# Layer turn of a graph network: old rows and biases of four tiles added by one wide product each

## The chip, the cores and the metric

The kernel runs on 1 core of one Trainium2 chip. The metric is the device time of one launch in microseconds (us), the median of the runs shown: before the change 7408.9 us (3 runs, 7406.33 to 7413.53).

## The reference, cut to what matters

The kernel computes four stacked graph layers on 6250 nodes with 128 channels and 100000 edges. The change touches the first of them, L0, a graph transformer of four rounds (`N_LAYERS = 4`):

```python
h = x @ Wn + bn
for l in range(N_LAYERS):
    Q = h @ WQ[l] + bQ[l]; K = h @ WK[l] + bK[l]; V = h @ WV[l] + bV[l]
    scores = jnp.sum(Q[dst] * K[src], axis=-1) * scale
    e = jnp.exp(scores - seg_max[dst])
    messages = jax.ops.segment_sum((e / seg_sum[dst])[:, None] * V[src], dst, num_segments=n)
    out = messages @ WO[l] + bO[l]
    h = _layernorm(h + out, ln_g[l], ln_b[l])
return h @ Wout + bout
```

All arithmetic here is float32. A node with no incoming edge gets no share of bV, so the bias that is added to h is bO for all nodes and bV @ WO for nodes with edges only.

## The kernel before, in words

**Tiles.** The 6250 rows are 49 tiles of 128 nodes (`T`), in an order that the kernel made itself (`k.perm`, `L.perm`). `k.h` holds the rows of the layer, `k.acc` the sums that the edge pass made (columns 0 to 127) and their denominators (column 128). Columns 129 to 256 of `k.acc` are free in this mode and are named `k.marks` (L3571); a row pair of them is used here.

**Order of the whole.** L3581: a loop of three rounds over `edge_pass` and `layer_turn` (so turns 1 to 3 are the same code), then one more `edge_pass` and one `layer_turn` with `last=True` (turn 4). Everything behind it (`place_rest`, `near_edges`, the later layers) follows in order. Each function is a stage: it ends in `close_stage` (L101), a reset of the DMA semaphores on POOL and a barrier of all engines. So whatever a turn takes longer or shorter moves the end of the kernel.

**A turn.** `layer_turn` (L2720) goes through the 49 tiles in 13 groups of `GB = 4` (L2686; the last group has one tile). For group g:

1. ACT `weigh` (L2832) multiplies the sums by the reciprocal denominators into `a`.
2. PE transposes the four tiles of `a` into `turned_ps` (L2787), ACT copies them to `at` (L2849).
3. PE adds up `sum_ps[g % 2]` (L2799 to L2801), per tile three products of 128 columns: the identity times the old rows, the marks (two rows: "has an edge" and "one") times `k.add2` (two rows: bV @ WO and bO), and `at` times `wvo`, the product of WV and WO.
4. DVE takes mean and variance (L2914, L2917), ACT the root (L2842), DVE the scale (L2905, L2907), ACT the normalised rows (L2858), DVE applies gain and offset (L2930, L2932) and stores them to `k.h` (`stored`).
5. In turns 1 to 3 POOL scatters each stored tile to the table in HBM with one indirect DMA (L2963). In turn 4 POOL has no such work; it gathers the 49 tiles of x with indirect DMAs from the start of the turn (L2954).
6. PE transposes the new rows (L2815), ACT copies them (L2867), PE multiplies them by `w2` (L2823), DVE adds the bias (L2947, in turn 4 L2943 and L2945).

The engines run these steps in queues written out by hand: in step i of the loop PE does the transposes of group i, the sums of i-1, the transposes of new rows of i-3 and the products of i-4. The order on PE is fixed, so a wait in the sums holds all that is behind it.

**The start of a turn.** SP loads the marks of all tiles with one DMA into two partitions of `k.acc` (L2756; `marked`). PE transposes the weights and makes bV @ WO as one row (L2762), DVE copies it into row 0 of `k.add2` (L2881; `raw`), and row 1, bO, was fetched during the edge pass by `fetch_layer` on ACT's queue (L2707). PE's first sum waits for `marked` and `made` (L2793, L2794).

**Names.** `own` is a helper that counts DVE's own instructions, so that DVE can wait for its own writes. `FETCHED` (L2687) is the number of DMAs that SP waits for at L2447, at the end of the edge pass.

Of the kernel before, what the change touches and what calls it, by code (L numbers as in the profile page):

```python
# [23 lines left out]
P = 128  # L24
# [3 lines left out]
NPAD = T * P  # L28
# [2655 lines left out]


GB = 4  # L2686
FETCHED = {False: 10, True: 8}  # L2687
NGB = -(-T // GB)


def group_tiles(g):
# [4 lines left out]
def fetch_layer(act, m, k, I, l, last):  # L2696

    def matrix(n, j):
        return I[f"L0_gnn_{n}"][ds(j, 1)].rearrange("a i j -> (a i) j")

    def column(n, j):
        return I[f"L0_gnn_{n}"][ds(j, 1)].rearrange("a (p n) -> (a p) n", n=1)

    act.dma_start(k.raw["WV"][:], matrix("WV", l)).then_inc(m["fetched"], 16)
    act.dma_start(k.raw["WO"][:], matrix("WO", l)).then_inc(m["fetched"], 16)
    act.dma_start(k.bv[:], column("bV", l), allow_slow_non_contiguous=True).then_inc(m["fetched"], 16)
    act.dma_start(k.add2[1:2], I["L0_gnn_bO"][ds(l, 1)]).then_inc(m["fetched"], 16)  # L2707
    for n, o in (("ln_g", k.gb), ("ln_b", k.bb)):
        act.dma_start(o[:], I[f"L0_gnn_{n}"][ds(l, 1)].rearrange("a n -> (a n)").partition_broadcast(P)).then_inc(m["fetched"], 16)
    if last:  # L2710
        act.dma_start(k.w1[:], I["L0_gnn_Wout"]).then_inc(m["fetched"], 16)
        act.dma_start(k.b1[:], row(I["L0_gnn_bout"])).then_inc(m["fetched"], 16)
        return
    act.dma_start(k.raw["WQ"][:], matrix("WQ", l + 1)).then_inc(m["fetched"], 16)
    act.dma_start(k.raw["WK"][:], matrix("WK", l + 1)).then_inc(m["fetched"], 16)
    act.dma_start(k.bq[:], column("bQ", l + 1), allow_slow_non_contiguous=True).then_inc(m["fetched"], 16)
    act.dma_start(k.bk[:], column("bK", l + 1), allow_slow_non_contiguous=True).then_inc(m["fetched"], 16)


def layer_turn(nc, k, last, x_d):  # L2720

    made = ["WV"] if last else ["WV", "WQ", "WK"]
    W2 = P if last else P + 1
    with ExitStack() as s:
        m = open_stage(nc, s, ["own", "shares", "raw_ps", "raw", "made_ps", "made", "spread_ps", "weighed", "turned_ps", "turned",
                               "summed_ps", "stat", "rooted", "scale", "normed", "stored", "rows_ps", "rows", "out_ps", "out_taken",
                               "scattered", "marked"] + [f"kept{g}" for g in range(NGB if last else 0)])
        wt = {n: buf(nc, s, f"wt_{n}", [P, P + 1]) for n in made}
        wvo = buf(nc, s, "wvo", [P, P])
        wz = buf(nc, s, "wz", [P, P + 1])  # L2730
        bz = buf(nc, s, "bz", [1, P + 1])
        bias = buf(nc, s, "lt_bias", [P, W2])
# [20 lines left out]
        with nc.Block() as block:  # L2753
            @block.sync
            def _(sp):
                sp.dma_start(k.marks[0:2], k.marks_d.rearrange("r (t p) -> r t p", p=P)).then_inc(m["marked"], 16)  # L2756

            @block.tensor
            def _(pe):
                for r, n in enumerate(made):  # L2760
                    pe.transpose(w_ps[:, r, :], k.raw[n][:], k.ident[:])
                pe.matmul(w_ps[0:1, 3, :], k.bv[:], k.raw["WO"][:], start=True, stop=True).then_inc(m["raw_ps"], 1)  # L2762
                pe.wait_ge(m["raw"], 2)
                pe.matmul(made_ps[:, 0, :], wt["WV"][:, 0:P], k.raw["WO"][:], start=True, stop=True).then_inc(m["made_ps"], 1)

                def next_weights():
# [13 lines left out]
                for i in range(NGB + 4):  # L2780
# [8 lines left out]
                    if 0 <= i - 1 < NGB:  # L2789
                        g = i - 1  # L2790
                        pe.wait_ge(m["turned"], g + 1)
                        if g == 0:
                            pe.wait_ge(m["made"], 1)  # L2793
                            pe.wait_ge(m["marked"], 16)  # L2794
                        if g >= 2:
                            pe.wait_ge(m["normed"], g - 1)
                        for j, t in enumerate(group_tiles(g)):
                            o = sum_ps[g % 2][:, j, :]
                            pe.matmul(o, k.ident[:], k.h[:, t, :], start=True, stop=False)  # L2799
                            pe.matmul(o, k.marks[0:2, t, :], k.add2[0:2], start=False, stop=False)  # L2800
                            mm = pe.matmul(o, at[g % 2][:, j, :], wvo[:], start=False, stop=True)  # L2801
                        mm.then_inc(m["summed_ps"], 1)
                        if g == 0:
                            next_weights()
                        if g == 1:
                            spread_bias()
# [63 lines left out]
            def _(dve):  # L2870
# [7 lines left out]
                dve.reciprocal(share[:], den[:]).then_inc(m["shares"], 1)  # L2878
                dve.wait_ge(m["raw_ps"], 1)
                dve.tensor_copy(wt["WV"][:, 0:P], w_ps[:, 0, :]).then_inc(m["raw"], 1)  # L2880
                dve.tensor_copy(k.add2[0:1], w_ps[0:1, 3, :]).then_inc(m["raw"], 1)  # L2881
                dve.wait_ge(m["made_ps"], 1)
                dve.tensor_copy(wvo[:], made_ps[:, 0, :]).then_inc(m["made"], 1)
                for r, n in enumerate(made[1:]):
# [65 lines left out]
            if last:  # L2950
                @block.gpsimd
                def _(pool):
                    for t in range(T):
                        pool.indirect_dma_start(k.x[:, t, :], None, x_d, bass.IndirectOffsetOnAxis(k.perm[:, t:t + 1], 0),  # L2954
                                                bounds_check=N - 1, oob_is_err=False).then_inc(m[f"kept{t // GB}"], 16)

            if not last:
                @block.gpsimd
                def _(pool):
                    for t in range(T):  # L2960
                        if t % GB == 0:
                            pool.wait_ge(m["stored"], t // GB + 1)
                        pool.indirect_dma_start(k.table_d, bass.IndirectOffsetOnAxis(k.perm[:, t:t + 1], 0), k.h[:, t, :], None  # L2963
                                                ).then_inc(m["scattered"], 16)
                    pool.wait_ge(m["scattered"], 16 * T)
# [291 lines left out]
def take_nodes(nc, k, I, deg, dn, list_d):  # L3257

    with ExitStack() as s:
# [39 lines left out]
        with nc.Block() as block:  # L3299
# [60 lines left out]
            def _(dve):  # L3360
# [13 lines left out]
                dve.wait_ge(m["marks_ps"], 1)  # L3374
                dve.tensor_copy(rows[:], small[0:T, 2, :]).then_inc(m["marks"], 1)
                dve.memset(k.acc[:, :, 0:P + 1], 0.0)
                dve.memset(k.add2[:], 0.0)
                dve.memset(k.x[:], 0.0)
                dve.wait_ge(m["loaded"], 16 * 7)
                for i, parts in enumerate((k.parts2, k.parts3)):  # L3380
# [105 lines left out]
def gnn_kernel(nc, I, out_d):  # L3486
    with ExitStack() as c:
# [84 lines left out]
        with ExitStack() as s:  # L3572
            k.raw = {n: buf(nc, s, f"raw_{n}", [P, P]) for n in ("WQ", "WK", "WV", "WO")}
            k.bq = buf(nc, s, "bq", [P, 1])
            k.bk = buf(nc, s, "bk", [P, 1])
            k.bv = buf(nc, s, "bv", [P, 1])
            k.add2 = buf(nc, s, "add2", [P, P])
            k.gb = buf(nc, s, "ln_g", [P, P])
            k.bb = buf(nc, s, "ln_b", [P, P])
            take_nodes(nc, k, I, L.deg, dn, listed[0])  # L3580
            with nc.Fori(0, k.layers - 1) as l:  # L3581
                edge_pass(nc, k, "attend", k.table_d, NPAD, P, *listed[0:3], dn.sched, fetch=(I, l, False), sort=(so, l), dn=dn)
                layer_turn(nc, k, False, I["x"])
            edge_pass(nc, k, "attend", k.table_d, NPAD, P, *listed[0:3], dn.sched, fetch=(I, k.layers - 1, True), sort=(so, k.layers - 1), dn=dn)
            layer_turn(nc, k, True, I["x"])
        place_rest(nc, k, so, L.sched, chunks)
        near_edges(nc, k, so, chunks, sweeps)
        with ExitStack() as s:
# [61 lines left out]
```

## Time and profile before

| | before |
|---|---|
| median of 3 runs | 7408.9 us |
| lowest, highest | 7406.33, 7413.53 us |
| span of the profiled execution | 10258.0 us |
| its mean granted TensorE clock | 0.709 of full speed |
| PE busy | 5437.6 us, 53% of the span |
| weight loads (PEld) busy | 4358.8 us, 42% |
| DVE busy | 4372.6 us, 43% |
| ACT busy | 2633.3 us, 26% |
| POOL busy | 4650.8 us, 45% |
| instructions | 129339 |

The profiled execution has no time of its own beside its span; the span is that of 129339 recorded instructions and is 38% above the median of the runs. No engine is busy for much more than half of it: the kernel is a chain of stages with different limits. A float32 product shows as two matmul records and two weight loads on PE (a transpose as one), so "x8" in a timeline row of L2823 is four products. The granted clock is given as a share of full speed: 1.00 is 2.4 GHz, 0.50 is 1.2 GHz.

### The profile page before, as it was taken

The numbers are of one execution on the slowest core, as the hardware profiler recorded it, in microseconds if no ns is written. First come the engines' busy times: TensorE is split into PE (matmuls) and PEld (weight loads), VectorE is DVE, ScalarE is ACT, GpSimd is POOL, SyncE is SP. The second block draws the span as 40 slices with busy tenths as digits, with TensorE's granted clock in tenths as the row PEclk, the third lists the DMA queues.
The fourth block names the chain that finished last, engine by engine and source line by source line (L and its number), as shares of the span: only waits on it lengthen the run. The fifth ranks groups of instructions, "written<-read, shape, count | busy, mean of one in ns | idle before, by whom it ended". The sixth has DMA issues, their size and how long they took to land. (4 is left out here: it accounts for less than half of the span.)

```text
span 10258.0 us, 129339 instructions
## 1 busy us (share of the span) xinstructions
PE 5437.6 (53%) x28962; PEld 4358.8 (42%) x28963; DVE 4372.6 (43%) x13513; ACT 2633.3 (26%) x7476; POOL 4650.8 (45%) x4878
## 2 busy tenths in 40 slices
PE   4404555554555555455645454444444455886888
PEld 3203444443444444444534343322222234776777
DVE  7503444424444334444334443344444454444444
ACT  0102222232222222222322222213333333333111
POOL 1473444434444444444444445244445444444554
PEclk8556777767777667777667777666666666887888
DMA  4202222112222122222122222122222213222222
GB/s 155 69 0 60 57 56 59 54 47 56 57 55 56 42 61 55 57 58 56 33 68 57 55 57 54 32 85 67 68 68 70 69 49 91 61 62 56 65 66 58
DMA packets 404676, 615.62 MB, mean 60 GB/s; under 512 B 213466, under 2 KB 255993, under 8 KB 403884
## 3 DMA queue, kind: packets, MB, share of 16 engines
q0 software_dynamic: 169952, 363.29, 13.1%
q1 hardware_dynamic: 211126, 200.20, 7.0%
q10 hardware_dynamic: 23130, 47.29, 1.4%
q14 instruction: 345, 2.83, 0.1%
q8 instruction: 123, 2.02, 0.1%
HBM read 528.32 MB, written 82.09 MB: 60 GB/s over the span
## 5 line engine op out<-in xcount | busy, mean ns | idle before, releaser
L1973 POOL DMA_INDIRECT rows<-table_d,meta x2432 | 2308.2, 949 | 1648.2 <-ACT weighted_rows L2140 835.2
L2037 PE MATMUL ps_total<-weighted_rows,ident 128*128 128x129 f32 (+1 forms) x6464 | 1700.6, 417 | 2122.2 <-issue 1604.1
L2037 PEld LDWEIGHTS ps_total<-weighted_rows,ident 128*128 128x128 f32 x6464 | 1329.3, 270 | 2529.7 <-issue 2423.2
L2369 DVE SCALAR_TENSOR_TENSOR prod<-rows,q_rows 128x129 f32<-128x129 f32 x2432 | 695.4, 294 | 1510.9 <-issue 1346.1
L1973 POOL DMA_INDIRECT rows<-pairs_d,meta x800 | 769.9, 962 | 781.3 <-DVE once_weighted L2429 526.6
L2073 PE MATMUL dense_sums<-x_rows,dense_power_t 128*128 128x129 f32 x3528 | 593.5, 317 | 662.8 <-issue 293.2
L2158 ACT COPY dense_power_t<-dense_turned 128x512 f32<-128x512 f32 x504 | 264.8, 525 | 2371.5 <-PE dense_turned L2064 1658.7
L2073 PEld LDWEIGHTS dense_sums<-x_rows,dense_power_t 128*128 128x128 f32 x3528 | 528.6, 227 | 703.6 <-issue 580.6
L2140 ACT ACTIVATE weighted_rows<-rows,power 128x129 f32<-128x129 f32 x2432 | 733.3, 389 | 18.4 <-PE ps_total L2037 14.6
L1532 POOL DMA_INDIRECT tile_rows<-table_d,tile_halves x441 | 416.2, 944 | 427.3 <-PE tile_sums L1783 294.2
L2193 ACT ACTIVATE weighted_rows<-once_weighted,of_relation 128x136 f32<-128x136 f32 x1600 | 488.0, 393 | 454.6 <-DVE once_weighted L2429 422.7
L1532 POOL DMA_INDIRECT tile_rows<-made_d,tile_halves x441 | 416.7, 945 | 378.0 <-PE tile_sums L1783 245.6
L1979 POOL DMA_INDIRECT list_out_d<-sort_stretch,sort_idx x72 | 74.8, 1039 | 1111.7 <-DVEq L2321 1111.7
L2250 DVE CUSTOM_DVE_ANT_0 dense_masked<-dense_scores,dense_masked,dense_least 128x896 f32<-128x896 f32 x252 | 289.7, 1150 | 499.6 <-issue 229.0
L1773 PE MATMUL tile_sums<-near_rows,sums 128*128 128x129 f32 x2352 | 366.3, 293 | 170.1 <-issue 166.7
L2064 PE MATMUL dense_turned<-ident,dense_masked 128*128 128x128 f32 x1764 | 318.3, 301 | 217.4 <-issue 138.2
L2372 DVE TENSOR_TENSOR src_store<-rows,q_rows 128x128 f32<-128x128 f32 x800 | 209.9, 291 | 516.3 <-issue 499.3
L2053 PE MATMUL dense_scores<-sums,dense_asked_t 128*128 128x512 f32 x512 | 317.2, 704 | 161.0 <-DVE dense_least L2250 61.7
L1773 PEld LDWEIGHTS tile_sums<-near_rows,sums 128*128 128x128 f32 x2352 | 314.1, 202 | 202.7 <-issue 201.4
L1783 PE MATMUL tile_sums<-tile_rows,sums 128*128 128x129 f32 x1764 | 339.2, 357 | 103.9 <-issue 103.1
L2064 PEld LDWEIGHTS dense_turned<-ident,dense_masked 128*128 128x128 f32 x1764 | 225.3, 153 | 340.4 <-issue 199.2
L1783 PEld LDWEIGHTS tile_sums<-tile_rows,sums 128*128 128x128 f32 x1764 | 314.6, 267 | 128.5 <-issue 128.4
(700 smaller groups left out, 9515.6 us busy)
## 6 DMA issues: line engine op xcount, KB each, us to landing
dense_masked<-dense_masks_d SPq DMA_DIRECT2D x252, 448.0 KB
rows<-table_d,meta POOLq DMA_INDIRECT x2432
dense_masks_d<-unmasked ACTq DMA_DIRECT2D x9, 3136.0 KB
src_store<-near_window_d SPq DMA_DIRECT2D x50, 384.0 KB
near_window<-near_window_d SPq DMA_DIRECT2D x48, 384.0 KB
rows<-pairs_d,meta POOLq DMA_INDIRECT x800
tile_rows<-table_d,tile_halves POOLq DMA_INDIRECT x441
tile_rows<-made_d,tile_halves POOLq DMA_INDIRECT x441
```

The costliest lines, as they stand in the source:

```text
L1532: pool.indirect_dma_start(rows[b][:, c, 0:P], None, table_d, bass.IndirectOffsetOnAxis(meta[:, t, c:c + 1], 0)).then_inc(got[b] if t < T - ...
L1773: pe.matmul(total[:, q, 0:P + 1], spare[:, q, c, :], near_rows[q][:, c, :], start=(c == 0), stop=False)
L1783: mm = pe.matmul(total[:, q, 0:P + 1], spare[:, q, NEAR + c, :], rows[t % RB][:, c, :], start=False, stop=(c == FARC - 1))
L1973: pool.indirect_dma_start(rows[q][:, j, 0:width], None, table_d, bass.IndirectOffsetOnAxis(meta[q][:, j, number:number + 1], 0)).then_inc( ...
L2037: mm = pe.matmul(total[:, q, ds(part, 1), 0:W].rearrange("p a w -> p (a w)"), k.ident[:], wide[:, j % WS, :], start=False, stop=True, skip ...
L2053: pe.matmul(dense_ps[:, 0, :].rearrange("p (t c) -> p t c", c=P), asked_t[:], xt[:, t0:t0 + 4, :], start=True, stop=True)
L2064: mm = pe.transpose(power_ps[:, j * P:(j + 1) * P], masked[u % 2][:, c * P:(c + 1) * P], k.ident[:])
L2073: mm = pe.matmul(sum_ps[:, 0:P + 1], power_t[h][:, j, :], k.x1[:, u * UNIT + 4 * h + j, :], start=(h == 0 and j == 0), stop=(h == 1 and j ...
L2140: ins = act.activation(wide[:, j, :], rows[q][:, j, :], ACT.Copy, scale=power[q][:, 0, j + 1:j + 2])
L2193: ins = act.activation(wide[:, j % WS, r * HW:(r + 1) * HW], once[:, j].rearrange("p h d -> p (h d)"), ACT.Copy, scale=of_relation[q][:, j ...
L2250: dve.tensor_tensor_reduce(masked[u % 2][:], dense_ps[:].rearrange("p b c -> p (b c)")[:, 0:UW], masked[u % 2][:], 1.0, least[:, u:u + 1], ...
L2369: own(dve.scalar_tensor_tensor(prod[:, j % 2, :], rows[q][:, j, :], -1.0, query, ALU.mult, ALU.mult, accum_out=score[:, j, :]))
```

## The change

Old rows and biases of the four tiles of a group are added by one product of 512 columns each, into the four quarters of one PSUM bank. For the biases this takes a block matrix: tile j of the group has its two marks in partitions 32j and 32j+1, and `add4` holds the two bias rows of tile j in the same partitions, in columns of tile j alone; all else in it is zero. The contraction runs over `BROWS` = 98 partitions. `add4` and the marks are therefore set to zero by POOL at the start of each turn, then SP loads marks and bO with nine DMAs in place of one (and of the one on ACT's queue in the edge pass), and DVE copies the bV @ WO row four times. The product with `wvo` stays one per tile.

```diff
-FETCHED = {False: 10, True: 8}
+FETCHED = {False: 9, True: 7}
+BROWS = 32 * (GB - 1) + 2
...
-    act.dma_start(k.add2[1:2], I["L0_gnn_bO"][ds(l, 1)]).then_inc(m["fetched"], 16)
...
+        add4 = buf(nc, s, "lt_add", [P, GB, P])
...
             @block.sync
             def _(sp):
-                sp.dma_start(k.marks[0:2], k.marks_d.rearrange("r (t p) -> r t p", p=P)).then_inc(m["marked"], 16)
+                sp.wait_ge(m["unmarked"], 2)
+                of_group = k.marks_d[:, 0:(NGB - 1) * GB * P].rearrange("r (g j p) -> r j g p", j=GB, p=P)
+                for j in range(GB):
+                    sp.dma_start(k.marks[32 * j:32 * j + 2, 0:NGB - 1, :], of_group[:, j]).then_inc(m["marked"], 16)
+                    sp.dma_start(add4[32 * j + 1:32 * j + 2, j, :], I["L0_gnn_bO"][ds(l, 1)]).then_inc(m["marked"], 16)
+                sp.dma_start(k.marks[0:2, NGB - 1, :], k.marks_d[:, (NGB - 1) * GB * P:NPAD]).then_inc(m["marked"], 16)
...
-                pe.matmul(w_ps[0:1, 3, :], k.bv[:], k.raw["WO"][:], start=True, stop=True).then_inc(m["raw_ps"], 1)
-                pe.wait_ge(m["raw"], 2)
+                pe.matmul(w_ps[0:BROWS, 3, :], k.bv[:].to_broadcast([P, BROWS]), k.raw["WO"][:], start=True, stop=True).then_inc(m["raw_ps"], 1)
+                pe.wait_ge(m["raw"], 1)
...
-                            pe.wait_ge(m["marked"], 16)
+                            pe.wait_ge(m["marked"], 16 * (2 * GB + 1))
+                            pe.wait_ge(m["raw"], 2)
                         if g >= 2:
                             pe.wait_ge(m["normed"], g - 1)
-                        for j, t in enumerate(group_tiles(g)):
-                            o = sum_ps[g % 2][:, j, :]
-                            pe.matmul(o, k.ident[:], k.h[:, t, :], start=True, stop=False)
-                            pe.matmul(o, k.marks[0:2, t, :], k.add2[0:2], start=False, stop=False)
-                            mm = pe.matmul(o, at[g % 2][:, j, :], wvo[:], start=False, stop=True)
+                        n = len(group_tiles(g))
+                        pe.matmul(sum_ps[g % 2][:, 0:n, :], k.ident[:], k.h[:, g * GB:g * GB + n, :], start=True, stop=False,
+                                  skip_group_check=True)
+                        pe.matmul(sum_ps[g % 2][:, 0:n, :], k.marks[0:BROWS, g, :], add4[0:BROWS, 0:n, :], start=False, stop=False,
+                                  skip_group_check=True)
+                        for j in range(n):
+                            mm = pe.matmul(sum_ps[g % 2][:, j, :], at[g % 2][:, j, :], wvo[:], start=False, stop=True, skip_group_check=True)
...
-                dve.tensor_copy(k.add2[0:1], w_ps[0:1, 3, :]).then_inc(m["raw"], 1)
+                for j in range(GB - 1):
+                    if j == 0:
+                        dve.wait_ge(m["unmarked"], 2)
+                    own(dve.tensor_copy(add4[32 * j:32 * j + 1, j, :], w_ps[32 * j:32 * j + 1, 3, :]))
+                own.wait()
+                dve.tensor_copy(add4[BROWS - 2:BROWS - 1, GB - 1, :], w_ps[BROWS - 2:BROWS - 1, 3, :]).then_inc(m["raw"], 1)
...
              @block.gpsimd
             def _(pool):
+                    pool.memset(add4[:], 0.0).then_inc(m["unmarked"], 1)
+                    pool.memset(k.marks[:, 0:NGB, :], 0.0).then_inc(m["unmarked"], 1)
```

Beside this `k.add2` and its clearing before the first layer are dropped, and `layer_turn` is given the inputs and the layer's number.

## Rows read from the trace of the kernel before

**Rows 1.** Windows: the four turns, each up to the next stage (busy us, clock, DMA).

```profile
2117.90:2235.80 117.90, 96.11 (x503) 76.45 (x503) 45.24 (x176) 50.62 (x139) 48.16 (x49) 0.77 0.09 29
3561.00:3682.70 121.70, 102.48 (x503) 82.27 (x503) 45.55 (x177) 50.60 (x139) 47.94 (x49) 0.71 0.08 28
5012.00:5130.00 118.00, 102.94 (x503) 82.83 (x503) 45.55 (x177) 51.26 (x139) 47.88 (x49) 0.71 0.08 28
6449.90:6600.40 150.50, 98.79 (x497) 79.54 (x497) 52.84 (x184) 51.37 (x139) 48.84 (x49) 0.68 0.08 22
```

**Rows 2.** Windows inside turns 1 and 3: PE, PEld, DVE, ACT, POOL busy; clock.

```profile
2134.00:2143.00 9.00, 9.00 (x30) 6.76 (x30) 1.49 (x11) 3.15 (x9) 0.00 (x0) 0.50 0.00 1
2158.00:2164.00 6.00, 6.00 (x43) 5.03 (x42) 3.40 (x14) 4.04 (x12) 3.67 (x5) 1.00 0.12 39
...
5079.00:5089.00 10.00, 10.00 (x37) 8.21 (x36) 2.56 (x13) 3.73 (x11) 4.96 (x5) 0.50 0.12 39
```

**Rows 3.** Timeline, PE in turn 1 at clock 1.00: one group (start us, us).

```profile
2158.76 0.39 PE L2799 MATMUL lt_sum<-h_rows,ident 128*128 128x128 f32 x2
2159.08 0.48 PE L2800 MATMUL lt_sum<-add,sums 2*128 2x128 f32 x2
2159.82 0.39 PE L2799 MATMUL lt_sum<-h_rows,ident 128*128 128x128 f32 x2
2163.42 1.06 PE L2823 MATMUL lt_out<-wz,lt_ht 128*128 128x129 f32 x8
2164.75 0.39 PE L2799 MATMUL lt_sum<-h_rows,ident 128*128 128x128 f32 x2
```

**Rows 4.** Timeline, PE in turn 1 at clock 0.50: two tiles of group 0.

```profile
2124.49 0.64 PE L2799 MATMUL lt_sum<-h_rows,ident 128*128 128x128 f32 x2
2126.36 0.63 PE L2799 MATMUL lt_sum<-h_rows,ident 128*128 128x128 f32 x2
```

**Rows 5.** Timeline, PE: products of 512 columns in edge passes, fast and slow.

```profile
5331.49 1.13 PE L2053 MATMUL dense_scores<-sums,dense_asked_t 128*128 128x512 f32 x2 [1.31 <-DVE dense_least L2250]
5332.46 0.81 PE L2055 MATMUL dense_scores<-sums,dense_asked_t 128*128 128x384 f32 x2
...
2289.70 2.08 PE L2053 MATMUL dense_scores<-sums,dense_asked_t 128*128 128x512 f32 x2 [1.53 <-DVE dense_least L2250]
2291.57 1.49 PE L2055 MATMUL dense_scores<-sums,dense_asked_t 128*128 128x384 f32 x2
```

**Rows 6.** POOL's scatters of turns 1 to 3 (line L2963: duration; idle time before).

```profile
L2963 POOL DMA_INDIRECT table_d<-h_rows,perm_in x147: 963/969/1187, 2144.8 to 5120.8; - x147
  issue: 38.6, 120
```

**Rows 7.** Start of a turn: DMA issues, a POOL memset, a DMA's landing (last number, us).

```profile
2117.92 0.78 SPq L2756 DMA_DIRECT2D sums<-marks_d  x1
L2707 ACTq DMA_DIRECT2D add<-in_L_gnn_bO x4: 486/488/536, 816.5 to 5149.9; - x4
L3302 POOL MEMSET dense_same<- 128x1600 f32 x1 | 1.4, 1431 | 7.8 <-POOLq L3564 7.8
tile_packed<-list_out_d SPq DMA_DIRECT2D x28, 31.5 KB, 2.2
```

**Rows 8.** Timeline, turn 4: a PE record, POOL's last gather, DVE's return.

```profile
6495.94 0.37 PE L2801 MATMUL lt_sum<-wvo,lt_at 128*128 128x128 f32 x1 [2.43 <-issue]
...
6513.21 0.99 POOL L2954 DMA_INDIRECT x_rows<-in_x,perm_in  x1 [0.30 <-issue]
...
6519.77 0.89 DVE L2914 BATCH_NORM_STATS2 lt_stats<-lt_sum 128x6 f32<-128x128 f32 x4 [52.01 <-remote]
```

**Rows 9.** Timeline, DVE: a late resumption in turn 1; the stage after turn 3.

```profile
2206.02 0.89 DVE L2914 BATCH_NORM_STATS2 lt_stats<-lt_sum 128x6 f32<-128x128 f32 x4 [7.04 <-DMA em_x<-in_x]
...
5129.98 0.10 DVE L1905 MEMSET rows<- 128x16 f32 x2 [1.63 <-PEq L104]
```

More of the change, by code:

```diff
@@ L2717, in fetch_layer, with layer_turn @@
     act.dma_start(k.bk[:], column("bK", l + 1), allow_slow_non_contiguous=True).then_inc(m["fetched"], 16)
-def layer_turn(nc, k, last, x_d):
+def layer_turn(nc, k, I, l, last):
+    x_d = I["x"]
     made = ["WV"] if last else ["WV", "WQ", "WK"]
@@ L2726, in layer_turn @@
                                "summed_ps", "stat", "rooted", "scale", "normed", "stored", "rows_ps", "rows", "out_ps", "out_taken",
-                               "scattered", "marked"] + [f"kept{g}" for g in range(NGB if last else 0)])
+                               "scattered", "marked", "unmarked"] + [f"kept{g}" for g in range(NGB if last else 0)])
         wt = {n: buf(nc, s, f"wt_{n}", [P, P + 1]) for n in made}
         wvo = buf(nc, s, "wvo", [P, P])
+        add4 = buf(nc, s, "lt_add", [P, GB, P])
         wz = buf(nc, s, "wz", [P, P + 1])
@@ L2959, in _ @@
                 def _(pool):
+                    pool.memset(add4[:], 0.0).then_inc(m["unmarked"], 1)
+                    pool.memset(k.marks[:, 0:NGB, :], 0.0).then_inc(m["unmarked"], 1)
                     for t in range(T):
@@ L3376, in _ @@
                 dve.memset(k.acc[:, :, 0:P + 1], 0.0)
-                dve.memset(k.add2[:], 0.0)
                 dve.memset(k.x[:], 0.0)
@@ L3576, in gnn_kernel @@
             k.bv = buf(nc, s, "bv", [P, 1])
-            k.add2 = buf(nc, s, "add2", [P, P])
             k.gb = buf(nc, s, "ln_g", [P, P])
@@ L3582, in gnn_kernel @@
                 edge_pass(nc, k, "attend", k.table_d, NPAD, P, *listed[0:3], dn.sched, fetch=(I, l, False), sort=(so, l), dn=dn)
-                layer_turn(nc, k, False, I["x"])
+                layer_turn(nc, k, I, l, False)
             edge_pass(nc, k, "attend", k.table_d, NPAD, P, *listed[0:3], dn.sched, fetch=(I, k.layers - 1, True), sort=(so, k.layers - 1), dn=dn)
-            layer_turn(nc, k, True, I["x"])
+            layer_turn(nc, k, I, k.layers - 1, True)
         place_rest(nc, k, so, L.sched, chunks)
```

## The prediction, made before the changed kernel was run

> **What bounds the kernel now.** I read the page first: no engine is busy for much over half of the span, so the question is which one sets the pace inside the four turns. The windows over each turn [rows 1] give 117.9, 121.7, 118.0 and 150.5 us, 508 us of the profiled span of 10258.0. PE is busy for 96 to 103 us of each, no other engine for more than 53. The windows inside a turn [rows 2] show PE busy in every microsecond, at clock 0.50 (1.2 GHz) 16 to 25 us into turn 1 and at 1.00 (2.4 GHz) 40 us into it; in turn 3 it stood at 0.50 once more, 67 us in. So in most of a turn PE's own work sets the pace.
>
> What that work is, the timeline shows. At clock 1.00 the first product of group 4 starts at 2158.76 and that of group 5 at 2164.75 [rows 3]: a period of 5.99 us. One tile of sums takes 2159.82 - 2158.76 = 1.06 us, four take 4.24, and the other 1.75 us are the two sets of transposes and the four products of L2823. At clock 0.50 a tile takes 1.87 us [rows 4], a group of sums 7.48.
>
> Two other things bound it. POOL's scatters in turns 1 to 3 take 0.969 us and 38.6 / 120 = 0.32 us of issue before each [rows 6], so 4 x 1.29 = 5.16 us a group: PE can't get faster than that for long, since the turn ends only when all 49 are out. And DVE comes back late now and then: at 2206.02 it had been idle for 7.04 us and the row names a DMA, not PE, whose sums it takes up [rows 9]. In turn 4 it is far stronger: while POOL gathers without a pause (to 6514.2), PE issues one record at a time, 2.43 us of idle before one of 0.37, and DVE comes back at 6519.77 after 52.01 us [rows 8]. I take both for late instructions; the rows show the lateness, not the cause.
>
> **The change part by part, for one full group.** It removes six of twelve products. The identity product becomes one of 512 columns. Edge passes have such products: 5332.46 - 5331.49 = 0.97 us fast, 2291.57 - 2289.70 = 1.87 us slow [rows 5]. The marks' product has 98 rows in place of 2; there is no such row. Its ends are 0.97 (its columns, rows being free) and 1.64 us (four narrow ones at 2159.82 - 2159.08 = 0.74 less one identity product's 0.32, so about 0.41 each, as now); I take 0.97, since the wide row has 128 partitions. The four products with wvo then stand one behind another as those of L2823 do, 1.06 us for four [rows 3], slow twice that, 2.12. Sum of a group, fast: 0.97 + 0.97 + 1.06 = 3.00 us for 4.24, so 1.24 less; slow: 1.87 + 1.87 + 2.12 = 5.86 for 7.48, 1.62 less. A whole fast group becomes 4.75 us on PE, and in turns 1 to 3 POOL's 5.16 is longer: there the gain is 5.99 - 5.16 = 0.83.
>
> **The start of a turn.** Added on the path to `marked`: POOL clears 512 + 13 x 128 = 2176 elements a partition, at 1431 / 1600 ns each [rows 7] 1.95 us. SP waits for it, with nothing else queued behind. Then nine issues: before, one of 98 row pieces took 0.78 us, one of a single row 0.49 [rows 7]. Four with 24 pieces I put at 0.6, four of bO at 0.49, the last at 0.5: 4.9 us (ends 4.4 and 7.0, nine times either row). Landing 2.2 us, from a load of 31.5 KB [rows 7] (ends 1.5, were it a third less, and 4.4, were it double under POOL's gathers). From 2117.92 that gives 2127.0, where the first sum started at 2124.49 [rows 4]: 2.5 us late (ends 1.3 and 6.8). Behind this wait PE holds the transposes of group 2, then ACT and DVE; all shift by it.
>
> Costed at nothing: DVE's four row copies and their wait for the memsets (till about 2119.9; they end some 1.2 us later, 3 us ahead of PE's first sum even as it was; uncovered they would cost that 1.2), the 98-column weight load for bV @ WO, and the DMA that leaves ACT's queue (0.49 us, in the edge pass, off its path). The clearing in turn 4 stands in front of POOL's gathers and moves the starved stretch by its 1.95 us; the marks' wait is hidden behind that stretch.
>
> **Sum.** Turns 1 to 3, each: +2.5 at the start; three slow groups -4.9 (from 2124.49 on, at 7.48 and some 1.6 for the rest, they reach to about 2152); nine fast full groups, of which the first five gain 0.83, -4.2, and four in the second half gain nothing, since there DVE's returns set the pace (if they don't, 3.3 more). Together -6.6, three times -19.8. Turn 4: +1.95, one slow group -1.6, eight fast ones at 1.24, -9.9 (POOL is done by then): -9.6. In all -29.4 us, against the profiled span 10258.0 a fall to 10228.6. That span is 38% above the median of the runs; the durations inside a turn are those of engines, so I carry the difference over one to one: 7408.9 - 29.4 = 7379.5, rounded to 7380. A measurement can tell about 0.2%, 15 us, from no change.
>
> **Rivals.** *(a) The wide product is used in full*: fewer instructions on PE end the late returns, all nine fast groups gain, the delay is 2.0. Turns 1 to 3: -4.9 - 7.5 + 2.0 = -10.4 each; in all -41, 7368. For it: PE issues 72 products fewer per turn. Against: the late engine in rows 9 is DVE, whose instructions don't get fewer. Chance 0.16.
>
> *(b) A new bound takes it*: POOL's scatters, now back to back, hold the engines' instructions as the gathers do in turn 4 [rows 8]. PE's gain at full clock is lost in turns 1 to 3, and the start costs 4.5: -0.4 each; only turn 4's -9.6 is left, -11, 7398. For it: the 52.01 us of rows 8. Against: in turn 1 POOL was 61% busy in the window of 6 us in which nothing was late [rows 2]. The Trainium skill, page "Runtime: NRT & Kernel Launch", section "Instruction fetch mechanics", says that each sequencer fetches its next block of instructions through a DMA queue of its own and that this is mostly hidden. By the rule alone this case should cost next to nothing and (a) be right; rows 8 and 9 speak against its "hidden". Chance 0.26.
>
> *(c) Slower: PE's clock.* It was 0.50 until some 25 us into turn 1 and again late in turn 3 [rows 2]. PE now gets pauses that it had not: the wait for `marked`, and 5.16 - 4.75 = 0.4 us in each group behind POOL. If it then stays low, a group takes 5.86 + 2 x 1.75 = 9.4 us where I count 5.16, 4.2 more. The forecast's 29.4 are gone after 7 such groups over all turns, and 15 us on the far side after 10.5. With four a turn: 16 x 4.2 = 67, so +38, 7447. For it: turn 3 did so by itself. Against: 0.4 in 5.16 leaves PE 92% busy. The Trainium skill, "TensorE: Matmul & The Clock Gate", section "HAM oscillation — how this bites in real kernels", says that pauses between bursts of products send the clock back to half. The trace has one such fall in turn 3, and none in the rows of full work. Chance 0.10.
>
> *(d) The change doesn't do what it says*: what a product costs lies in its columns, which stay the same, and the wide ones take as long as four narrow ones, 4.24 in all. Then only the starts count: 3 x 2.5 + 1.95 = +9.5, 7418. Against: rows 5, 0.97 for 512 columns beside 4 x 0.32 for the identity's four. Chance 0.06.
>
> **How the numbers follow.** The forecast has 0.42, with a range of its own of 7370 to 7391 (start and second half at either end). Faster by over 15 us (below 7394): the forecast, (a) and a fifth of (b), 0.63. Within 0.2%: the rest of (b), (d), 0.27. Slower: (c), 0.10. The range 7361 to 7406 takes in (a) and (b) with the bounds of the start and leaves out (c), (d) and the outermost part of (a).
>
> **What the changed profile would show.** The lines of L2799 and L2800 have 104 records each for the 52 groups (392 now), with 512 columns. The period of the first products at clock 1.00 is 5.1 to 5.2 us in turns 1 to 3, and 4.75 in turn 4. POOL's waits for h_rows get short, its waits for issue stay at 0.32. The first sum of a turn starts 9 us after the turn and not 6.6. The windows of rows 1 become some 111, 115, 111 and 141 us. I am wrong if the periods stay near 6 (then (b) or (d), told apart by the duration of the wide record), if the first sum is later than 11 us, or if clock 0.50 stands in more than the first four groups (then (c)).

## The result, and the profile after

The changed kernel took 7312.5 us, the median of 4 runs (7307.9 to 7316.4), beside 7411.2 us (7406.3 to 7417.9, 4 runs) for the kernel before: a ratio of 0.986 with an interval of 0.9848 to 0.9872, 98.7 us less. The forecast was 29.4 less, so the sign was right and the gain over three times as large. A single launch is now and then drawn out by hundreds of us or more (8272.1 us among the four of start_alone, whose median without it is 7311.3, and 9887.5 among the ten of rows_64), and the ratios leave such launches out.

The profiled execution of before that stands ahead of the prediction (span 10258.0 us) was a drawn-out one. A second one of the same kernel, below named *before again*, has a span of 7381.4 us. What follows compares with that one. First the top of the page of the changed kernel.

```profile
span 7314.8 us, 128253 instructions
PE 4737.9 (65%) x28386; PEld 3901.0 (53%) x28387; DVE 4310.6 (59%) x13524; ACT 2620.7 (36%) x7476; POOL 4676.6 (64%) x4886
```

Windows of the changed kernel, the four turns and the first 10 us of sums in turn 1, which answer to [rows 1, 2] (stretch; its length; busy us and instructions of PE, PEld, DVE, ACT, POOL; granted clock; DMA share; GB/s):

```profile
1691.80:1785.20 93.40, 64.00 (x359) 47.25 (x359) 46.16 (x180) 50.47 (x139) 51.85 (x51) 0.80 0.11 36
2689.20:2781.80 92.60, 63.83 (x359) 47.35 (x359) 46.42 (x181) 50.46 (x139) 51.15 (x51) 0.80 0.11 36
3687.70:3776.80 89.10, 63.92 (x359) 47.72 (x359) 46.45 (x179) 50.42 (x139) 51.89 (x51) 0.81 0.11 37
4681.90:4760.60 78.70, 65.25 (x354) 48.04 (x355) 54.79 (x188) 48.97 (x139) 51.81 (x51) 0.86 0.15 42
...
1698.00:1703.00 5.00, 5.00 (x12) 2.67 (x11) 0.00 (x0) 1.76 (x5) 0.00 (x0) 0.50 0.01 3
1703.00:1708.00 5.00, 5.00 (x28) 3.45 (x28) 2.37 (x14) 2.80 (x9) 0.00 (x0) 0.95 0.01 2
```

The same of before again, the four turns, then the stretch of turn 1 in which the clock rose, one of turn 2 25 to 34 us into it, and the one behind that, in which the clock rose:

```profile
1687.00:1790.10 103.10, 84.96 (x503) 68.69 (x503) 45.12 (x177) 51.82 (x139) 47.71 (x49) 0.85 0.10 33
2696.00:2807.40 111.40, 92.75 (x503) 74.76 (x503) 45.11 (x177) 51.92 (x139) 47.68 (x49) 0.78 0.09 30
3713.20:3821.40 108.20, 92.72 (x503) 74.72 (x503) 45.07 (x176) 51.93 (x139) 47.67 (x49) 0.79 0.09 31
4722.20:4830.90 108.70, 97.73 (x498) 78.77 (x499) 52.82 (x185) 51.59 (x139) 49.69 (x49) 0.74 0.12 31
...
1703.00:1707.00 4.00, 4.00 (x23) 3.05 (x21) 0.34 (x2) 3.15 (x9) 0.00 (x0) 0.88 0.00 0
2721.00:2730.00 9.00, 9.00 (x33) 7.21 (x32) 2.73 (x12) 3.52 (x11) 3.93 (x4) 0.50 0.08 29
2730.00:2734.00 4.00, 4.00 (x22) 3.17 (x21) 1.89 (x8) 3.85 (x11) 1.74 (x2) 0.83 0.05 16
```

The turns add up to 431.4 us before and 353.8 after: 77.6 less. All else together is 11.0 us longer after (6961.0 for 6950.0), so the spans differ by 66.6. In these two profiles and those of the eight other kernels below, this rest lies between 6950 and 6967 us and the turns add up to between 351 and 459, so nearly all that tells one kernel from another lies in the turns. PE's busy time in a turn fell by 21 to 33 us, POOL's rose by some 4 at most: the gain is PE's. It comes in two ways. The clock rose 5 us after the first sum (the window from 1703.00 to 1708.00 has 0.95 in the mean), where in turn 2 of before again it was still 0.50 in the window that ends 34 us into the turn, with PE busy in all of it. And a group at full clock is shorter, as PE's timeline in turn 1 after the change shows, group 0 at clock 0.50 and a later one at 1.00, answering to [rows 3, 4] (start, us, operation):

```profile
1698.52 2.05 PE L2807 MATMUL lt_sum<-h_rows,ident 128*128 128x512 f32 x2
1700.35 1.91 PE L2809 MATMUL lt_sum<-lt_add,sums 98*128 98x512 f32 x2
1702.06 1.76 PE L2812 MATMUL lt_sum<-wvo,lt_at 128*128 128x128 f32 x8
...
1730.01 1.02 PE L2807 MATMUL lt_sum<-h_rows,ident 128*128 128x512 f32 x2
1730.87 1.02 PE L2809 MATMUL lt_sum<-lt_add,sums 98*128 98x512 f32 x2
1731.73 1.05 PE L2812 MATMUL lt_sum<-wvo,lt_at 128*128 128x128 f32 x8
1732.63 0.60 PE L2826 MATMUL lt_rows<-ident,h_rows 128*128 128x128 f32 x4
```

From start to start: 0.86 + 0.86 + 0.90 = 2.62 us for a group's sums, where [rows 3] gave 4.24. The period of a group is 4.38 us (DVE takes up the sums of two groups in turn 1 at 1724.07 and 1728.45, with 0.89 us of waiting for PE before each).

The start of turn 1 in the timeline (POOL's clearing, the first and last of SP's nine issues, PE's second set of transposes), answering to [rows 7]:

```profile
1692.17 0.53 POOL L2978 MEMSET lt_add<- 128x512 f32 x1 [16.44 <-issue]
1692.63 1.50 POOL L2979 MEMSET sums<- 128x1664 f32 x1
1694.16 0.27 SPq L2762 DMA_DIRECT2D sums<-marks_d  x1
...
1696.80 0.25 SPq L2764 DMA_DIRECT2D sums<-marks_d  x1
...
1697.50 1.11 PE L2795 MATMUL lt_turned<-ident,lt_a 128*128 128x128 f32 x4 [1.85 <-ACT lt_a L2843]
```

The first sum starts 6.7 us into the turn (1698.52 - 1691.8), and 6.6 in before again (1693.59 - 1687.0): the marks' longer way cost next to nothing. POOL's scatters of turn 1, answering to [rows 6]:

```profile
L2983 POOL DMA_INDIRECT table_d<-h_rows,perm_in x49: 965/972/1519, 1710.7 to 1774.2; - x49
  issue: 14.6, 48
```

From the start of the first scatter (1710.7) to that of the last (1774.2) are 63.5 us and 48 steps. A step of 0.972 + 14.6 / 48 = 1.276 gives 61.2, and five scatters that took longer (up to 1.519 for 0.972) give the rest. The only idle time before a scatter is that of its issue, so POOL has no gap left. Turn 1 is 18.9 us to the first scatter, 63.5 to the start of the last and 11.0 from there to the end, 93.4 in all. PE's groups come every 4.38 us, faster than POOL's 4 x 1.276 = 5.10, so in turns 1 to 3 the bound is now POOL's, as forecast.

### The profile page after: what moved, and what is told of

Read it like the earlier page. It is cut to its first block and busy times, and to the rows that moved or that the text cites. A ratio compares the mean times of both kernels' runs of the same rounds, so it can differ in the third digit from the quotient of the medians.

```text
span 7314.8 us, 128253 instructions
## 1 busy us (share of the span) xinstructions
PE 4737.9 (65%) x28386; PEld 3901.0 (53%) x28387; DVE 4310.6 (59%) x13524; ACT 2620.7 (36%) x7476; POOL 4676.6 (64%) x4886
## 3 DMA queue, kind: packets, MB, share of 16 engines
q8 instruction: 119, 1.95, 0.1%
## 5 line engine op out<-in xcount | busy, mean ns | idle before, releaser
L2037 PE MATMUL ps_total<-weighted_rows,ident 128*128 128x129 f32 (+1 forms) x6464 | 1425.4, 380 | 652.7 <-ACT weighted_rows L2193 484.8
L2037 PEld LDWEIGHTS ps_total<-weighted_rows,ident 128*128 128x128 f32 x6464 | 1179.9, 235 | 897.7 <-issue 725.3
L2073 PE MATMUL dense_sums<-x_rows,dense_power_t 128*128 128x129 f32 x3528 | 622.0, 328 | 557.1 <-DVE dense_rows L2260 521.6
L2073 PEld LDWEIGHTS dense_sums<-x_rows,dense_power_t 128*128 128x128 f32 x3528 | 558.9, 238 | 598.2 <-issue 590.9
L2146 ACT ACTIVATE dense_shrink<-dense_least 128x1 f32<-128x1 f32 x252 | 74.0, 294 | 749.8 <-DVE dense_least L2250 749.8
L2064 PEld LDWEIGHTS dense_turned<-ident,dense_masked 128*128 128x128 f32 x1764 | 241.0, 159 | 163.7 <-ACT dense_power_t L2158 91.4
L1758 PE MATMUL near_gathered<-q_rows,near_hot 128*128 128x128 f32 x2352 | 275.7, 278 | 73.7 <-DVE near_hot L1622 73.7
L1758 PEld LDWEIGHTS near_gathered<-q_rows,near_hot 128*128 128x128 f32 x2352 | 271.4, 195 | 74.2 <-DVE near_hot L1622 67.9
L1991 PE MATMUL ps_total<-nothing,ident_bf 128*128 128x387 bf16 x160 | 67.6, 427 | 359.9 <-DVE nothing L2231 345.4
L1758 PE MATMUL near_gathered<-x_rows,near_hot 128*128 128x128 f32 x2352 | 275.5, 278 | 31.9 <-DVE near_hot L1622 31.9
```

Source lines behind the costliest of these rows:

```text
L1758: mm = pe.matmul(gathered[:, h, at:at + P], near_hot[i][:, c % 2, j, :], table[:, WIDE * c + j, 0:P], start=(j == 0), stop=(j == WIDE - 1) ...
L2037: mm = pe.matmul(total[:, q, ds(part, 1), 0:W].rearrange("p a w -> p (a w)"), k.ident[:], wide[:, j % WS, :], start=False, stop=True, skip ...
L2064: mm = pe.transpose(power_ps[:, j * P:(j + 1) * P], masked[u % 2][:, c * P:(c + 1) * P], k.ident[:])
L2073: mm = pe.matmul(sum_ps[:, 0:P + 1], power_t[h][:, j, :], k.x1[:, u * UNIT + 4 * h + j, :], start=(h == 0 and j == 0), stop=(h == 1 and j ...
```

## The experiments

Each is an edit of the kernel before unless said otherwise. "Turns" are the four turns of its profiled execution. In the rows `sums` is the buffer of the marks and `add` is `k.add2`.

**before_again.** The kernel before, unchanged.

> The kernel before, unchanged, profiled once more, since its first profile had a span of 10258 us where the changed kernel's is 7314.8. Clock theory (the wide products let TensorE's clock rise earlier, and that is the larger part of the 98.7 us): a span near 7410, turns 1 to 3 of 110 to 118 us each, and clock 0.50 for at least the first 25 us of PE's sums in every turn, although PE has no pause. Work theory (the gain is the products' own time, and the profile of before was drawn out elsewhere): the clock is at 1.00 within 10 us of the first sum, and a group takes 6.0 us from then on.

Its run was 7382.9 us, its turns 103.1, 111.4, 108.2, 108.7. In turn 4 nothing is starved: DVE's waits are PE's sums, as this row of its timeline shows, where [rows 8] had 52.01 us.

```profile
4788.51 0.89 DVE L2914 BATCH_NORM_STATS2 lt_stats<-lt_sum 128x6 f32<-128x128 f32 x4 [1.77 <-PE lt_sum L2801]
```

So [rows 8, 9] belong to that one drawn-out execution and not to the kernel. The group's period at full clock is 5.99 us here too, so [rows 3] do belong to it.

**start_alone.** The changed kernel with its marks, block matrix and start, but twelve products of 128 columns per group, in the old order.

```diff
-                        pe.matmul(sum_ps[g % 2][:, 0:n, :], k.ident[:], k.h[:, g * GB:g * GB + n, :], ...)
-                        pe.matmul(sum_ps[g % 2][:, 0:n, :], k.marks[0:BROWS, g, :], add4[0:BROWS, 0:n, :], ...)
+                        for j, t in enumerate(group_tiles(g)):
+                            o = sum_ps[g % 2][:, j, :]
+                            pe.matmul(o, k.ident[:], k.h[:, t, :], start=True, stop=False)
+                            pe.matmul(o, k.marks[0:BROWS, g, :], add4[0:BROWS, j, :], start=False, stop=False)
+                            mm = pe.matmul(o, at[g % 2][:, j, :], wvo[:], start=False, stop=True)
```

> The new start (clearing, nine DMAs, block matrix, marks' product over 98 rows) with products of 128 columns only, twelve a group as before. Clock theory: nothing raises the clock, so the start's cost alone shows: 2 to 10 us slower than before, turns at 0.50 as long as in before. If the 98 rows in place of 2 were what raises the clock: 30 us or more faster. Work theory: 2 to 10 us slower.

Measured: 7314.2 us, ratio 0.9874 (0.9847 to 0.9901); turns 91.6, 92.6, 88.7, 77.7, period 4.45. That is the full change's time with none of its wide products for the old rows and biases. PE's timeline at clock 1.00:

```profile
1715.53 0.39 PE L2809 MATMUL lt_sum<-h_rows,ident 128*128 128x128 f32 x2
1715.75 0.39 PE L2810 MATMUL lt_sum<-lt_add,sums 98*128 98x128 f32 x2
1715.98 0.39 PE L2811 MATMUL lt_sum<-wvo,lt_at 128*128 128x128 f32 x2
1716.20 0.39 PE L2809 MATMUL lt_sum<-h_rows,ident 128*128 128x128 f32 x2
```

Every narrow product takes 0.22 to 0.23 us, a tile 0.67, where it was 1.06 in [rows 3]. Not only the bias product got cheaper, which now has 98 rows, but also the two of 128 rows on either side of it, which did not change. So what was paid for before stands between products, not in them.

**rows_wide.** Only the old rows by one wide product; the biases stay two rows.

```diff
+                        pe.matmul(sum_ps[g % 2][:, 0:n, :], k.ident[:], k.h[:, g * GB:g * GB + n, :], start=True, stop=False, ...)
                         for j, t in enumerate(group_tiles(g)):
-                            pe.matmul(o, k.ident[:], k.h[:, t, :], start=True, stop=False)
```

> Only the old rows as one product of 512 columns per group; start and marks' products as before (nine products a group). Clock theory: the clock rises nearly as early as in the changed kernel; 50 to 90 us faster than before. Work theory: PE's own saving alone, (4 x 0.32 - 0.97) to 0.5 us a group, 52 groups: 15 to 30 us faster.

Measured: 7404.6 us, ratio 0.9996 (0.9984 to 1.0008): nothing. Its timeline at clock 1.00:

```profile
1742.37 1.02 PE L2798 MATMUL lt_sum<-h_rows,ident 128*128 128x512 f32 x2
1743.32 0.48 PE L2802 MATMUL lt_sum<-add,sums 2*128 2x128 f32 x2
1743.73 0.49 PE L2803 MATMUL lt_sum<-wvo,lt_at 128*128 128x128 f32 x2
1746.56 0.60 PE L2817 MATMUL lt_rows<-ident,h_rows 128*128 128x128 f32 x4
```

The last row is the first transpose behind the group. From start to start a group's sums take 1746.56 - 1742.37 = 4.19 us, where twelve narrow ones took 4.24. The group still goes from 128 rows to 2 and back four times, eight changes in all, and a narrow product stands at 0.41 us where start_alone's took 0.22.

The clock did not even hold once it was up. Two windows of turn 1, one behind the other, with PE busy in all of both:

```profile
1760.00:1764.00 4.00, 4.00 (x26) 2.96 (x25) 3.39 (x13) 2.79 (x8) 1.49 (x2) 1.00 0.11 36
1764.00:1768.00 4.00, 4.00 (x21) 3.43 (x20) 1.47 (x9) 2.01 (x6) 3.08 (x4) 0.73 0.14 49
```

All four turns of this profile fall back like this several times and add up to 459.1 us. It is that of the slowest of the kernel's ten runs, 7428.0 us.

**three_wide_first.** Tests the clock: three products of 512 columns that nobody reads, ahead of the first transposes of a turn.

```diff
                 pe.matmul(made_ps[:, 0, :], wt["WV"][:, 0:P], k.raw["WO"][:], start=True, stop=True).then_inc(m["made_ps"], 1)
+                for _w in range(3):
+                    pe.matmul(out_ps[:].rearrange("p a b -> p (a b)")[:, 0:512], k.ident[:], k.h[:, 0:GB, :], start=True, stop=True)
```

> The kernel before with three more products of 512 columns (identity times old rows, into a PSUM bank that is not used yet) at the start of each turn, ahead of the first transposes; nothing reads them. That adds 3 x 1.87 = 5.6 us of PE work per turn at 1.2 GHz, of which 2 to 4 lie beside other waits. Clock theory: the clock is at 1.00 when the sums begin and stays, and the kernel is 20 to 70 us faster than before in spite of the added work; if the clock falls back under the narrow products, 0 to 15 us slower. Work theory: 5 to 20 us slower.

Measured: 7367.8 us, ratio 0.9947 (0.9927 to 0.9967); turns 101.7, 100.7, 98.9, 95.5, together 396.8, period 5.99. Two windows of turn 1, the wide products and the first sums:

```profile
1693.00:1697.00 4.00, 4.00 (x8) 1.72 (x7) 0.69 (x3) 0.55 (x2) 0.00 (x0) 0.64 0.03 8
1701.00:1710.00 9.00, 9.00 (x54) 6.77 (x53) 2.23 (x14) 4.27 (x14) 0.00 (x0) 1.00 0.00 0
```

The clock is up before the sums begin and stays up with the row changes, in all four turns. Beside before again that is worth 431.4 - 396.8 = 34.6 us of turns, with the same sums. It is worth this although the unread products delay the first sum: it starts 9.1 us into turn 1 (1700.0 - 1690.9), for 6.6.

**rows_128.** The kernel before with the bias products over all 128 rows. The rows beyond the two are zeros, written once in an early stage.

```diff
-                            pe.matmul(o, k.marks[0:2, t, :], k.add2[0:2], start=False, stop=False)
+                            pe.matmul(o, k.marks[0:P, t, :], k.add2[0:P], start=False, stop=False)
...
-                dve.memset(k.acc[:, :, 0:P + 1], 0.0)
+                dve.memset(k.acc[:, :, 0:2 * P + 1], 0.0)
```

> The kernel before with its old start, its single marks DMA and its twelve products of 128 columns; only the bias product runs over all 128 partitions in place of 2 (the others hold zeros, cleared once ahead of the first layer). Row-count theory (a product of 2 rows between products of 128 rows costs PE about 0.19 us at each of the two changes, and keeps the clock low for longer): three products of a tile take 0.67 us at clock 1.00 in place of 1.06, the clock is at 1.00 within 5 us of the first sum, and the kernel is as fast as the changed one, 7300 to 7320. Start theory (the clearing, the later marks or the block matrix made start_alone fast): as before, 7385 to 7425.

Measured: 7315.0 us, ratio 0.9871 (0.9848 to 0.9893); turns 92.5, 92.9, 88.6, 77.9. The whole gain, with the product's row count as the only thing changed in a turn. Windows and timeline of turn 1:

```profile
1703.00:1707.00 4.00, 4.00 (x21) 4.00 (x20) 0.00 (x0) 1.76 (x5) 0.00 (x0) 0.50 0.01 4
1708.00:1713.00 5.00, 5.00 (x41) 4.29 (x40) 2.82 (x16) 3.31 (x10) 0.00 (x0) 1.00 0.00 0
```

```profile
1704.64 0.63 PE L2799 MATMUL lt_sum<-h_rows,ident 128*128 128x128 f32 x2
1705.92 0.63 PE L2799 MATMUL lt_sum<-h_rows,ident 128*128 128x128 f32 x2
...
1735.50 0.39 PE L2799 MATMUL lt_sum<-h_rows,ident 128*128 128x128 f32 x2
1736.17 0.39 PE L2799 MATMUL lt_sum<-h_rows,ident 128*128 128x128 f32 x2
```

A tile takes 1.28 us at clock 0.50 and 0.67 at 1.00, for 1.87 and 1.06 in [rows 3, 4]; and the clock is up 5 us after the first sum, with no added product ahead of it to bring that about.

**rows_64.** The same edit with 64 rows.

```diff
-                            pe.matmul(o, k.marks[0:P, t, :], k.add2[0:P], start=False, stop=False)
+                            pe.matmul(o, k.marks[0:64, t, :], k.add2[0:64], start=False, stop=False)
```

> As rows_128, with a bias product of 64 rows. Row-count theory, if any difference from 128 rows costs the change: 1.06 us a tile and about the time of before, perhaps with an earlier clock (7360 to 7410). If only few rows cost it: 0.67 us a tile, 7300 to 7320. Start theory: as before.

Measured: 7397.3 us, ratio 0.9988 (0.9972 to 1.0004); period 6.0. The timeline at clock 1.00:

```profile
1745.28 0.39 PE L2799 MATMUL lt_sum<-h_rows,ident 128*128 128x128 f32 x2
1745.60 0.49 PE L2800 MATMUL lt_sum<-add,sums 64*128 64x128 f32 x2
1746.01 0.49 PE L2801 MATMUL lt_sum<-wvo,lt_at 128*128 128x128 f32 x2
1746.34 0.39 PE L2799 MATMUL lt_sum<-h_rows,ident 128*128 128x128 f32 x2
```

A tile takes 1.06 us, as with two rows. So 64 rows beside 128 are a change, 98 beside 128 are none; where between the two the line lies was not tried. The Trainium skill, page "TensorEngine Tiling (Array Packing)", section "Key Properties", says that going from one tiling mode of the array to another drains TensorE, and the modes that it lists have 128, 64 or 32 rows. The runs fit that, if a product of 2 or 64 rows works in a mode of fewer rows and one of 98 in that of 128; no trace names the mode. What a change costs is measured next.

**two_rows_grouped.** Two rows again, but per group the four identity products first, then the four of two rows, then the four with wvo.

```diff
                         for j, t in enumerate(group_tiles(g)):
                             pe.matmul(quarter(j), k.ident[:], k.h[:, t, :], start=True, stop=False, ...)
+                        for j, t in enumerate(group_tiles(g)):
                             pe.matmul(quarter(j), k.marks[0:2, t, :], k.add2[0:2], start=False, stop=False, ...)
+                        for j, t in enumerate(group_tiles(g)):
                             mm = pe.matmul(quarter(j), at[g % 2][:, j, :], wvo[:], start=False, stop=True, ...)
```

> The kernel before with the same twelve products of a group in another order: four of old rows, four of 2 rows, four with wvo. Row-count theory: the cost lies in the change of row count, two changes a group in place of eight, so a group of sums takes 12 x 0.223 + 2 x 0.19 = 3.05 us at clock 1.00 for 4.24, while the clock may still rise late; 7320 to 7370. If a product of 2 rows is slow by itself: 1.06 us a tile still, 7385 to 7425.

In this order the kernel does not compute the reference's sums, so it gives a price and not a remedy. Number, size and rows of the products are those of before. Measured: 7323.3 us, ratio 0.9886 (0.9862 to 0.9909); turns 97.0, 95.6, 93.2, 82.2, period 4.83. PE's timeline of one group:

```profile
1738.26 1.06 PE L2799 MATMUL lt_sum<-h_rows,ident 128*128 128x128 f32 x8
1739.24 1.16 PE L2801 MATMUL lt_sum<-add,sums 2*128 2x128 f32 x8
1740.33 1.16 PE L2803 MATMUL lt_sum<-wvo,lt_at 128*128 128x128 f32 x8
1741.32 0.60 PE L2817 MATMUL lt_rows<-ident,h_rows 128*128 128x128 f32 x4
```

3.06 us for the sums with two changes of the row count, where twelve products without any take 12 x 0.223 = 2.67. One change costs (3.06 - 2.67) / 2 = 0.19 us. The kernel before has eight: (4.24 - 2.67) / 8 = 0.20. The two agree, so it is the number of changes that is paid for, not the two-row product.

The clock goes the same way. Windows of turn 1, whose first sum starts at 1693.1:

```profile
1696.00:1700.00 4.00, 4.00 (x18) 3.11 (x18) 0.89 (x4) 0.00 (x0) 0.00 (x0) 0.50 0.00 0
1701.00:1706.00 5.00, 5.00 (x39) 4.52 (x37) 1.72 (x11) 3.43 (x11) 0.00 (x0) 0.96 0.00 2
```

In the four turns it rose 6.9 to 8.3 us after the first sum. With no change in the sums (the changed kernel, start_alone, rows_128) it took 2.6 to 5.2 us, and with eight a group (before again, rows_64) 10 to 37. Since the products are those of before, the changes between them keep the clock low for longer, and not the two rows by themselves.

**rows_128_act_clears.** rows_128 with the zeros written once by ACT in the same early stage, in place of DVE's longer clearing, with which turn 1 had begun only at 1696.8 us (before again: 1687.0).

```diff
+                act.activation(k.marks[:], k.ones[:].unsqueeze(1).to_broadcast([P, T, P]), ACT.Copy, scale=0.0)
```

> As rows_128, but the zeros in the unused partitions of the marks are written once by ACT, which waits at that point ahead of the first layer, in place of DVE, whose longer clearing made the stretch ahead of the first turn 5 us longer (1696.8 against 1691.8). Row-count theory: all of rows_128's gain and 4 to 6 us more, 7306 to 7313, a little below the changed kernel, which has no need of its block matrix, clearing and nine DMAs. Start theory: between before and the changed kernel.

Measured: 7307.2 us (7302.8 to 7309.7), ratio 0.9861 (0.9838 to 0.9883); turns 92.9, 92.6, 89.0, 77.8, turn 1 at 1688.7. Its median is 5 us below the changed kernel's 7312.5; their ranges overlap, and 5 us is under 0.2%. At least as fast, then, without the block matrix, the nine loads or any clearing in a turn.

**and_three_wide.** The last one with three unread wide products: two ahead of the first transposes of a turn, one behind them, to bring the clock up still earlier.

```diff
+                spare = lambda: pe.matmul(out_ps[:].rearrange("p a b -> p (a b)")[:, 0:512], k.ident[:], k.h[:, 0:GB, :], start=True, stop=True)
+                spare()
+                spare()
...
+                        if g == 0:
+                            spare()
```

> As rows_128_act_clears, with three products of 512 columns at the start of each turn that nothing reads: two ahead of the first transposes, one behind them. If the low clock still costs something in the first group of sums (slow products 0.427 us each, fast 0.223: 12 x 0.2 = 2.4 us), each turn begins its scatters 1 to 3 us earlier: 7298 to 7308. If the products delay the transposes, which they stand in front of, by as much: no difference, within 3 us of rows_128_act_clears.

Measured: 7308.8 us, ratio 0.9863 (0.9841 to 0.9886); turns 92.9, 93.0, 90.2, 77.6: no gain. The clock is up before the sums here too, but the two products stand in front of the transposes for 3.2 us, and the first sum starts 8.8 us into turn 1 (1701.4 - 1692.6) for 6.6 in rows_128_act_clears (1695.3 - 1688.7):

```profile
1695.24 3.37 PE L2765 MATMUL lt_out<-h_rows,ident 128*128 128x512 f32 x4
1698.44 0.60 PE L2790 MATMUL lt_turned<-ident,lt_a 128*128 128x128 f32 x4
```

## Why the prediction was wrong in size

Turn by turn the forecast was -6.6 three times and -9.6. The profiles have -9.7, -18.8, -19.1 and -30.0.

**The cause was another one.** The prediction credited the gain to six products fewer and to wide ones being cheap for their columns. Neither is worth anything by itself: start_alone has as many products as before and the full gain, rows_wide has a wide product and no gain. Four narrow products at 0.22 are 0.89 us and one wide one 0.86. What the change took away is the change of row count between products, by way of a matrix that happened to have 98 rows. In that, rival (d) was half right: what a product costs does lie in its columns. But then 0.32 and 0.41 per narrow one in [rows 3] were not products' prices; each held part of a change.

**The step "rows being free".** The price 0.97 for the marks' product was near (0.86 measured). The failure stands beside it, in the rest of the group: four with wvo at 1.06 (0.90 measured), a group's sum 3.00 (2.62). In turn 4 the forecast's period of 4.75 us came to 4.38 in the middle groups and 4.60 in the later ones, so at most 12 x 0.37, some 4 us, were missed there. In turns 1 to 3 it is nothing, since POOL's floor holds: 5.16 was forecast, 4 x 1.276 = 5.10 measured.

**The step "three slow groups -4.9".** It took the stretch at clock 0.50 as given and only made its groups cheaper. The clock came up 5 us after the first sum instead, because the row changes were gone. This was the larger error: 4.9 us a turn, 1.6 in turn 4, were forecast for the whole slow stretch. Of the 77.6 us, 34.6 are what an early clock gives alone (three_wide_first), and the rest, 396.8 - 353.8 = 43.0, the changes at full clock. The split is fair to about 2 us a turn: three_wide_first loses 2.5 us to its late first sum, and the changed kernel about as much to a first group at half clock (12 x (0.427 - 0.223) = 2.4). By the timed runs it is 42 us (7410.0 to 7367.8) and 55 us (to 7312.5). Turn by turn, in the profiles, the clock is worth 1.4, 10.7, 9.3 and 13.2 us, the changes 8.3, 8.1, 9.8 and 16.8. The forecast's prices a group were near for the changes: 12 x 0.83 = 10 us against 8 to 10 in turns 1 to 3, and 12 x 1.24 = 14.9 against 16.8 in turn 4. But that is partly luck, since they stood for wide products and not for changes, and the sum applied them to five groups and eight.

**The steps resting on late instructions.** "Four in the second half gain nothing" and "starved until 6519.77" came from [rows 8, 9]. before_again has neither. By the prediction's own figure the first of them kept 3 x 3.3 = 9.9 us out of the sum. A profiled execution with its span 38% above the median of the runs should have warned more: its engines' durations held, its waits did not. Turn 4 was forecast at -9.6 and gave -30.0.

**The start.** Forecast +2.5, measured 0.1. SP's nine issues stood 0.33 us apart and took 0.23 to 0.27 each, where the nearest rows had 0.49 and 0.78, and the clearing was 2.03 us for 1.95. The chain of ACT and transposes, not `marked`, was still what released the first sum: the second set of transposes starts at 1697.50, 1.85 us after PE's last work, released by ACT, and the sum follows at 1698.52. Turn 4's clearing ahead of its gathers cost nothing visible.

**The rivals.** (a) rightly expected that all groups gain, but for reasons that were not there. (b), POOL starving the engines: POOL is back to back in turns 1 to 3, and DVE still took up the sums of turn 1 every 4.38 us or sooner to the last; nothing was starved. (c) had the right quantity and the wrong sign. It feared that pauses of PE would keep the clock low; what kept it low was PE's own work with changes in it, and the change took that away. Its reading was loose too: it saw one fall of the clock, in turn 3, "and none in the rows of full work", but that fall is a row with PE busy for 10.00 of 10.00 us [rows 2]. The same trace also has short falls in turns 1 and 2 (0.54 from 2194 to 2196, 0.56 from 3648 to 3650), there with PE idle for 0.24 and 0.82 us of the two. The Trainium skill, page "TensorE: Matmul & The Clock Gate", section "HAM oscillation — how this bites in real kernels", puts a falling clock down to pauses between bursts. Two profiles show no such pause: in before again turn 2 stayed at 0.50 with PE busy for 9.00 of 9.00 us, and in rows_wide the clock fell with PE busy for 4.00 of 4.00. A busy time of that kind takes in the 0.2 us of every change, though. If PE stands still in them, the page's account could hold, and nothing here shows whether it does.

**What stays open.** Why changes of the row count keep the clock at 0.50 was not found, nor why the clock then rises sooner in some turns than in others: before again needed 10 us from its first sum in turn 1 (1693.6 to about 1704.0), 29 in turns 2 and 3 and 37 in turn 4, and rows_wide, with its eight changes, was at 0.50 and 1.00 by turns within one turn, while before again, rows_64 and three_wide_first, with eight changes too, held 1.00 once they had it. That scatter fits the runs of before, 7380 to 7431 us in all measurements, beside 7308 to 7316 after, and would make up for the profiles differing by 66.6 us where the medians differ by 98.7: before again, with 7382.9, was among the fastest runs of its kernel. This was argued from the ranges, not measured turn by turn. What drew out the first profiled execution is not known either.

## What to carry to other kernels

Keep the number of contraction rows alike from product to product: a two-row bias product between products of 128 rows costs its neighbours more than itself, and padding it with zeros to 128 rows takes that away. Putting all such products together takes most of it away, but only where the sums allow that order; here they did not. Where a turn starts at half clock, look whether PE's work itself is of the kind that keeps it there before looking for pauses. Before resting a step on a wait, see that the profiled execution's span is near the median of the runs.

## What the runs showed of the hardware that was not expected

- A change between 128 rows and 2 or 64 costs 0.19 to 0.20 us on PE at clock 1.00 (float32 products of 128 columns). At 0.50 it is (1.87 - 1.28) / 2 = 0.30 us. Between 98 and 128 rows there is none.
- A float32 product of 128 columns takes 0.223 us at clock 1.00 and 0.427 at 0.50 when nothing changes, and as a quarter of a wide one 0.215 at clock 1.00.
- With eight such changes a group, the clock stayed at 0.50 for 10 to 37 us of sums in which the profile shows no pause (before again, rows_64); with two it rose in 7 to 8 us, and with none in 3 to 5. Once up, it held with the eight in (before again, rows_64, three_wide_first), but fell back in every turn of rows_wide.
